# The last chunk of a decoder layer's cross attention: the third chunk's projections in every second step, its gate and its expert slots three steps later, the second sort from step 199 on

## The chip, the cores and the metric

The kernel runs on one core of a Trainium2 chip (trn2), all in float32. The metric is the device time of one launch in microseconds (us). A core has five engines with an instruction queue each: PE (TensorE, matrix products), DVE (VectorE), ACT (ScalarE), POOL (GpSimd) and SP (SyncE, which here only issues DMAs). An engine works its own queue in the order in which it was written, and waits for the others at semaphores.

## What is computed

One decoder layer over 2048 tokens of width 256: linear attention with a residual and a layer norm; cross attention of 16 heads over 1601 keys with a residual and a layer norm; then a mixture of 16 experts, of which each token takes 4, beside a shared one, with a residual and a layer norm.

```python
x = _layernorm(x + _L0_attn_ref(x, ...))
x = _layernorm(x + _L0_xattn_ref(x, ctx_1024, ctx_1024, ...))
x = _layernorm(x + _L0_ffn_ref(x, ...))
# in the cross attention
scores = einsum('bhqd,bhkd->bhqk', Q, K) * scale
out = einsum('bhqk,bhkd->bhqd', softmax(scores), V)
return out @ Wo + bo
# in the mixture
probs = softmax(xf @ gate_w.T)
top_w, top_idx = top_k(probs, 4)        # weights divided by their sum
moe_out = einsum('ted,te->td', eout, combine)
shared = silu(xf @ sw1.T) * (xf @ sw3.T) @ sw2.T
```

## The kernel before

**Steps.** The cross attention is a loop of 208 steps. The queries are cut in four chunks of 512 (`c`), the heads in four groups of four, the keys in 13 tiles (`KT`), so that a chunk has 52 steps and step `s` is tile `kt = s % 13` of group `G = s // 13`. `at` is the step within its chunk; the last chunk is steps 156 to 207, its last group steps 195 to 207. In a step PE makes the scores of four heads (L1531), each into a bank of PSUM of its own, ACT takes their exponentials (L1273), and PE weighs the values with those of two steps before (L1545; L1559 in the last group). The maxima that a softmax needs are found ahead: two "units" of a step are products of PE (L1454) which DVE reduces (L1916, the short last ones of a group L1912). DVE has two such units' banks and PE fills the next only when one has been read. The units run 15 steps ahead, so the last are in step 192. In the last 15 steps DVE has no units.

**Work behind the scores.** What follows the attention of a chunk is spread over the steps of the next one, by the table `EXTRA`: behind the scores of a step, PE does one piece, and ACT copies it out. For the third chunk (`c == CHUNKS - 2`) these are four projections (`proj`, PE L1568, ACT L1169), one for each tile of 128 tokens, the turning of the normalised rows (`x2T`, PE L1576), the gate's products (`logits`, PE L1593) and two counts (`rank`, L1603 and L1606) of how many tokens each expert has got. POOL adds a projection to its rows a step later (`add_attention`, L1002), DVE takes mean and variance another step later (`attended_stats`, L1894 and L1895), POOL makes the inverse deviation (L837), and ACT and POOL normalise two tiles each (POOL L1013). DVE then does the gate in pieces, one in a step (`gate_centre` to `gate_share`), POOL adds up the choices (`third_chosen`), and after the second count DVE works out in which slot of the experts' input each choice goes (`open_more` to `all_slots`, L2143 at its end), and in which order the tiles of slots are to be worked (`order_tiles`, `place_owners`).

**The sort.** POOL writes each token's row to its slots in DRAM with indirect DMAs (`sorted_d`, L853), 128 rows each: 32 for the first two chunks (stage 0) and 16 for the third (stage 1), both within the last chunk's steps, by the table `SORT_AT`; 16 for the last chunk come much later. In POOL's program a scatter of step `s` stands behind a wait for the first score of that step (`ring_full`, `slot(s, 0) + 1`). The 16 of stage 1 go in rounds `j` of four tiles; ahead of each half round stand an iota and a copy (`mark`, L847 and L849) which write the row's place and weight into the rows, and for that first wait until the half's scatters of the round before have landed. POOL also issues the DMA of the order (`write_order`, L919) at step 201.

**The experts' stage.** Its loop has work items `i`, of which the first four are tiles of the shared expert and item 4 is the first of the experts. SP loads that tile's rows from `sorted_d` (L711), with a wait for all scatters of stages 0 and 1 ahead of the first load (L695). PE, at `i == 1`, does the last chunk's projection (L1646), and turns item 4's rows (L1690) right behind it.

Of the kernel before, what the change touches and what calls it, by code (L numbers as in the profile page):

```python
# [20 lines left out]
CHUNKS = SEQ // CHUNK  # L21
TPC = CHUNK // P
# [102 lines left out]
PAIR = 2  # L125
# [19 lines left out]
def decoder_layer(nc, a, out):  # L145
    with ExitStack() as ctx:
# [140 lines left out]
        proj = sb("proj", [P, TPC, DIM])  # L287
# [89 lines left out]
        for c in range(CHUNKS - 1):  # L377
            first = CHUNK_STEPS * (c + 1)
            if c == CHUNKS - 2:
                jobs = ([(12 + t, "proj", t) for t in range(TPC)]  # L380
                        + [(4, "rank", 0), (21, "x2T", 0), (22, "x2T", 1), (23, "logits", 0),
                           (32, "rank", 1)])
            else:
                jobs = ([(PROJ_AT[t], "proj", t) for t in range(TPC)]
                        + [(30, "x2T", 0), (32, "x2T", 1), (34, "logits", 0)])
            for at, what, which_one in jobs:
                assert first + at not in EXTRA
                EXTRA[first + at] = (what, (c, which_one))
# [99 lines left out]
                        NORMED_AT[i + 6] = [t - 1, t]  # L488
        SCATTER_AT = {14 + k: divmod(k, TPC) for k in range(TOPK * TPC)}
        SORT_AT = {}  # L490
        for stage, first, pace in ((0, 166, 0.8), (1, 196, 0.75)):
            for k in range(TOPK * STAGE_TILES[stage]):
                SORT_AT.setdefault(first + int(pace * k), []).append((stage, *divmod(k, STAGE_TILES[stage])))
        assert sum(len(rows) for rows in SORT_AT.values()) == GATE_FIRST * TOPK and max(SORT_AT) < STEPS
# [289 lines left out]
        def _(pool):  # L784
# [231 lines left out]
            for s in range(STEPS):  # L1016
                c, at = divmod(s, CHUNK_STEPS)
                if at == 2 * KT + 9:
                    divide(c, 0)
                if at == 9 and c >= 1:  # L1020
                    divide(c - 1, 1)
                if 1 <= c < CHUNKS - 1:
                    for t in range(TPC):
                        if at == PROJ_AT[t] + 1:
                            add_attention(c - 1, t)
                    if at == 27:
                        inverse_deviation(c_var, c_rstd, c - 1, TPC)
                    if at == 28:
                        normalise(c - 1, range(TPC))
                if c == CHUNKS - 1 and at == 18:  # L1030
                    inverse_deviation(c_var, c_rstd, c - 1, TPC)
                    make_shift(c - 1)
                if c == CHUNKS - 1 and at == 6:
                    first_slots()
                if s in SORT_AT:
                    if s == min(SORT_AT):
                        pool.wait_ge(sorted_cleared, 16 * len(CLEARS))
                    pool.wait_ge(ring_full, slot(s, 0) + 1)
                    for row in SORT_AT[s]:
                        sort_row(*row)  # L1040
                if c == CHUNKS - 1:
                    if 13 <= at < 13 + TPC:
                        add_attention(c - 1, at - 13)
                    if at in (18, 19):
                        normalise(c - 1, (PAIR + at - 18,))
                if c == CHUNKS - 1 and at == 30:
                    third_chosen()
                if s == CHUNK_STEPS * (CHUNKS - 1) + 45:
                    write_order(0)
# [21 lines left out]
        def _(act):  # L1071
# [184 lines left out]
            for s in range(STEPS):  # L1256
# [26 lines left out]
                    copy_logits(arg[0], n)  # L1283
                elif what == "rank":
                    copy_rank(arg[1], n)
                if c == CHUNKS - 1 and at in (19, 20):
                    normalise(c - 1, at - 19)
                if c >= 1 and at == (26 if c == CHUNKS - 1 else 39):
                    exp_gate(c - 1)
            copy_num(CHUNKS * GROUPS - 1)  # L1290

# [540 lines left out]
        def _(dve):  # L1832
# [496 lines left out]
            for s in range(STEPS):  # L2329
# [26 lines left out]
                    if at == 51:  # L2356
                        gate_chosen(c - 1)
                if c == CHUNKS - 1:
                    if 14 <= at < 14 + TPC:
                        attended_stats(c - 1, at - 14)  # L2360
                        if at == 13 + TPC:
                            add_eps(c_var)
                    if at == 25:
                        gate_centre(c - 1)
                    if at == 27:
                        gate_softmax(c - 1)
                    if at == 28:
                        gate_top(c - 1)
                    if at == 29:
                        gate_which(c - 1)  # L2370
                    if at == 30:
                        gate_hot(c - 1)
                    if at == 31:
                        gate_share(c - 1)
                    if at == 6:
                        open_tiles(0)
                    if at == 37:
                        dve.wait_ge(chosen_ready, CHUNKS - 1)
                        dve.wait_ge(slots_ready, 1)
                        open_more(1)  # L2380
                        reach_more(1)
                        slot_of_choice(1)
                        all_slots(1)
                    if at == 42:
                        order_tiles()
                        owners_by_count()
                        place_owners()
                        prepare_last()
# [95 lines left out]
```

## Time and profile before

| | us |
|---|---|
| median of 3 runs | 907.58 |
| lowest and highest | 907.54, 910.18 |
| the profiled execution, time | 907.53 |
| its span, first to last instruction | 905.6 |
| PE busy | 875.7 (97%) |
| DVE busy | 703.0 (78%) |
| ACT busy | 668.4 (74%) |
| POOL busy | 322.3 (36%) |
| granted TensorE clock, mean | 0.994 |

PE is busy nearly throughout, but a busy PE is not PE at its peak: the profile models where a pipelined product ends. In the chain that ended last, PE's lines have 79% of the span, DVE 12% and ACT 5%. The stage that the change touches runs from 625 us (step 168) to about 740 us (the experts' first tile); the experts' stage follows to the end. A step without other work takes 2.47 us up to step 192, and 1.9 to 2.0 us from step 195 on.

### The profile page before, as it was taken

What the parts mean: (1) busy time and instruction counts of PE and PEld (TensorE: products, weight loads), DVE (VectorE), ACT (ScalarE), POOL (GpSimd) and SP (SyncE); (2) the same over time, 40 slices, a digit from 0 to 9 for tenths busy, and PEclk for the clock granted to TensorE, in tenths of its full rate; (3) what the DMA queues carried; (4) which work ended last, traced back from release to release, by engine and by line L of the source; (5) the groups of instructions that cost most, each with busy time, mean ns of one, the idle gap of its engine ahead of it and who ended that gap; (6) DMA issues with size and microseconds to landing.
All of it is one profiled execution on the core that took longest, in us unless ns stands there. A gap on an engine that the chain in (4) does not pass through costs nothing.

```text
span 905.6 us, 19295 instructions
## 1 busy us (share of the span) xinstructions
PE 875.7 (97%) x6987; PEld 501.4 (55%) x6987; DVE 703.0 (78%) x1122; ACT 668.4 (74%) x1491; POOL 322.3 (36%) x385
## 2 busy tenths in 40 slices
PE   8999999999999999999999999999999999999995
PEld 5776776544444444444444444444444367888883
DVE  5336789899999998899998898998889446311587
ACT  4435664378888888888888788888888956677773
POOL 1916787630000001020000020005654644777674
PEclk9999999999999999999999999999999999999997
DMA  9307638403335221011011011011334743466795
GB/s 324 100 1 141 135 100 135 114 26 89 102 96 172 78 71 27 9 26 31 9 26 32 8 25 26 14 26 38 108 112 128 196 124 111 141 173 203 259 327 178
DMA packets 69781, 91.56 MB, mean 101 GB/s; under 512 B 15224, under 2 KB 52602, under 8 KB 69656
## 3 DMA queue, kind: packets, MB, share of 16 engines
q1 hardware_dynamic: 62008, 68.52, 27.0%
q0 software_dynamic: 6928, 18.82, 5.7%
q10 hardware_dynamic: 752, 2.98, 2.0%
q8 instruction: 58, 0.95, 0.5%
q14 instruction: 35, 0.29, 0.1%
HBM read 48.80 MB, written 39.40 MB: 97 GB/s over the span
## 4 chain that ended last, share of the span: by engine, by line
PE 79%; DVE 12%; ACT 5%; issue 2%; POOL 1%; DMA 1%; POOLq 0%; DVEq 0%; ACTq 0%
PE psum L1545 21%; PE psum L1454 17%; PE psum L1531 9%; PE psum L1728 9%; DVE mpart L1916 7%; PE psum L1746 4%; ACT region L1273 3%; PE psum L1374 2%; PE psum L1690 2%; PE psum L1339 2%; PE psum L1505 2%; PE psum L1471 2%; PE psum L1568 1%; PE psum L1347 1%; ACT region L1132 1%
## 5 line engine op out<-in xcount | busy, mean ns | idle before, releaser
L1273 ACT ACTIVATE region<-psum 128x512 f32<-128x512 f32 (+1 forms) x832 | 447.8, 610 | 77.1 <-PE psum L1531 63.3
L1916 DVE TENSOR_REDUCE mpart<-psum 128x2 f32<-128x1024 f32 x384 | 462.0, 1222 | 25.9 <-PE psum L1454 21.3
L1545 PE MATMUL psum<-region 128*32 128x256 f32 (+1 forms) x3120 | 248.8, 390 | 1.8
L1454 PE MATMUL psum<-kstack,qstack 63*128 63x512 f32 (+1 forms) x1024 | 211.2, 441 | 4.9 <-DVE mpart L1916 3.7
L1454 PEld LDWEIGHTS psum<-kstack,qstack 63*128 63x128 f32 x1024 | 88.1, 184 | 173.9 <-issue 123.8
L1531 PE MATMUL psum<-qstack,kstack 64*128 64x512 f32 (+1 forms) x832 | 174.1, 406 | 0.7 <-ACT region L1273 0.7
L1545 PEld LDWEIGHTS psum<-region 128*32 128x32 f32 (+1 forms) x3120 | 64.1, 108 | 107.6 <-issue 83.7
L1531 PEld LDWEIGHTS psum<-qstack,kstack 64*128 64x128 f32 (+1 forms) x832 | 111.2, 181 | 16.2 <-ACT region L1273 13.2
L997 POOL TENSOR_TENSOR attnT<-num_c,den_c 128x512 f32<-128x512 f32 x7 | 9.0, 1281 | 244.6 <-DMA den_c<-den_d 244.4
L928 POOL DMA_INDIRECT given_d<-y_out,x_in x79 | 77.3, 978 | 37.8 <-ACT y_out L1239 25.8
L1728 PE MATMUL psum<-w_all,xT_in 128*128 x316 | 81.6, 381 | 0.9 <-ACT xT_in L1217 0.5
L2284 DVE SCALAR_TENSOR_TENSOR act_h<-silu_h,psum 128x128 f32<-128x128 f32 x95 | 27.2, 287 | 68.6 <-ACT silu_h L1221 68.0
L1728 PEld LDWEIGHTS psum<-w_all,xT_in 128*128 128x128 f32 x316 | 53.9, 190 | 5.5 <-issue 1.3
L853 POOL DMA_INDIRECT sorted_d<-x_rows,slots x48 | 47.6, 992 | 25.5 <-PE psum L1531 14.2
L1132 ACT ACTIVATE region<-psum,small 128x64 f32<-128x64 f32 x128 | 27.9, 329 | 26.8 <-DVE small L1927 26.7
L1746 PE MATMUL psum<-w_all,actT 128*128 x158 | 47.2, 380 | 0.0
L1221 ACT ACTIVATE silu_h<-psum 128x128 f32<-128x128 f32 x85 | 23.6, 278 | 29.7 <-PE psum L1728 29.6
L1239 ACT ACTIVATE y_out<-psum,x_in 128x256 f32<-128x256 f32 x79 | 37.4, 474 | 7.6
L1217 ACT ACTIVATE xT_in<-psum 128x256 f32<-128x256 f32 x95 | 35.7, 377 | 6.5 <-PE psum L1690 6.3
L1912 DVE TENSOR_REDUCE mpart<-psum 128x8 f32<-128x528 f32 x32 | 22.7, 708 | 13.0 <-PE psum L1454 11.6
L1002 POOL TENSOR_TENSOR x_rows<-proj,x_rows 128x256 f32<-128x256 f32 x12 | 8.3, 688 | 65.2 <-ACT proj L1169 65.1
L837 POOL TENSOR_TENSOR rstd<-var_eps,half_neg 128x1 f32<-128x1 f32 (+1 forms) x20 | 13.2, 658 | 49.8 <-DVE var_eps L2002 37.0
(304 smaller groups left out, 1039.2 us busy)
## 6 DMA issues: line engine op xcount, KB each, us to landing
x_in<-sorted_d SPq DMA_DIRECT2D x79, 129.0 KB, 2.3
sorted_d<-x_in SPq DMA_DIRECT2D x6, 1548.0 KB, 7.9
given<-given_d SPq DMA_DIRECT2D x16, 512.0 KB, 5.8
qstack<-qparts_d SPq DMA_DIRECT2D x96, 64.0 KB, 2.3
qparts_d<-region SPq DMA_DIRECT2D x8, 512.0 KB, 3.0
kparts_d<-region SPq DMA_DIRECT2D x4, 800.5 KB, 9.3
kstack<-kparts_d SPq DMA_DIRECT2D x6, 400.2 KB, 10.2
kstack<-kparts_d ACTq DMA_DIRECT2D x6, 400.2 KB, 14.0
```

Source lines behind the costliest of these rows:

```text
L853: pool.indirect_dma_start(out=sorted_d[:, :], out_offset=bass.IndirectOffsetOnAxis(ap=slots[:, t, j:j + 1], axis=0), in_=row, in_offset=No ...
L928: pool.indirect_dma_start(out=given_d[:, :], out_offset=bass.IndirectOffsetOnAxis(ap=x_in[:, v % X_SLOTS, DIM:DIM + 1].bitcast(I32), axis= ...
L1132: ins = act.activation(qexp[:, i % 2, head], bank(i % 2)[:, head], ACT.Exp, bias=small[:, 32 * (i % 2) + h:32 * (i % 2) + h + 1])
L1217: act.activation(xT_in[:, i % 3, :], turn_bank("tile", i)[:, 0:DIM], ACT.Copy).then_inc(xT_copied, 1)
L1239: act.activation(y_out[:, v % Y_SLOTS, :], bank(2 + i % 2)[:, 0:DIM], ACT.Copy, scale=x_in[:, v % X_SLOTS, DIM + 1:DIM + 2]).then_inc(y_co ...
L1273: act.activation(prob[0:rows_of, s % 3, j, :], ring(n)[0:rows_of], ACT.Exp).then_inc(ring_read, 1)
L1454: mm = pe.matmul(bank(unit_bank(u) + side)[:, at * w:(at + 1) * w], qstack[rows_of, buffer(G), p, t * P:(t + 1) * P], kstack[rows_of, g * ...
L1531: pe.matmul(ring(n)[0:r], kstack[rows, g * PAIRS + p, kt * P:kt * P + r], qstack[rows, buffer(G), p, :], start=True, stop=True).then_inc(r ...
L1545: mm = pe.matmul(bank(NUM_BANK)[VW * j:VW * (j + 1), q], vals[0:r, g, kt, j, :], prob[0:r, s % 3, j, q], start=(kt == 0 and half == 0), st ...
L1728: mm = pe.matmul(bank(6 + i % 2)[:, 0:2 * HID], xT_in[:, i % 3, k * P:(k + 1) * P], part_of(kind, v, k), start=(k == 0), stop=(k == DK - 1))
L1746: pe.matmul(bank(2 + i % 2)[:, 0:DIM], actT[:, i % ACT_SLOTS, :], part_of(kind, v, DK), start=True, stop=True).then_inc(y_done, 1)
L1916: dve.tensor_reduce(mpart[:, G % 2, qt, :, p, n], both, X, ALU.max).then_inc(max_read, 1)
```

## The change

It moves work of the third chunk within the last chunk's steps. Nothing is added or left out.

| | before | after |
|---|---|---|
| projections on PE and ACT | steps 168, 169, 170, 171 | 168, 170, 172, 174 |
| POOL adds them | 169 to 172 | 169, 171, 173, 175 |
| DVE's statistics | 170 to 173 | 170, 172, 174, 176 |
| inverse deviation on POOL | 174 | 177 |
| normalising on POOL; on ACT | 174, 175; 175, 176 | 177, 178; 178, 179 |
| `x2T`, `x2T`, `logits` | 177, 178, 179 | 180, 181, 182 |
| DVE's gate, six pieces | 181 to 187 | 184 to 190 |
| `third_chosen` on POOL | 186 | 189 |
| second `rank` | 188 | 191 |
| `open_more` to `all_slots` on DVE | 193 | 196 |
| stage 1 sort on POOL, 16 scatters | 196 + int(0.75 k) | 199 + int(0.55 k) |

`order_tiles` (step 198), `write_order` (201), the load of the order (205) and stage 0's sort (166 to 190) keep their steps.

```diff
-                jobs = ([(12 + t, "proj", t) for t in range(TPC)]
-                        + [(4, "rank", 0), (21, "x2T", 0), (22, "x2T", 1), (23, "logits", 0),
-                           (32, "rank", 1)])
+                jobs = ([(12 + 2 * t, "proj", t) for t in range(TPC)]
+                        + [(4, "rank", 0), (24, "x2T", 0), (25, "x2T", 1), (26, "logits", 0),
+                           (35, "rank", 1)])
...
-        for stage, first, pace in ((0, 166, 0.8), (1, 196, 0.75)):
+        for stage, first, pace in ((0, 166, 0.8), (1, 199, 0.55)):
...
-                    if 14 <= at < 14 + TPC:
-                        attended_stats(c - 1, at - 14)
-                        if at == 13 + TPC:
-                            add_eps(c_var)
-                    if at == 25:
+                    for t in range(TPC):
+                        if at == 14 + 2 * t:
+                            attended_stats(c - 1, t)
+                    if at == 20:
+                        add_eps(c_var)
+                    if at == 28:
                         gate_centre(c - 1)
...
-                    if at == 37:
+                    if at == 40:
                         dve.wait_ge(chosen_ready, CHUNKS - 1)
                         dve.wait_ge(slots_ready, 1)
                         open_more(1)
```

PE's queue from the projection of step 169 to that of step 170, before. L1568 is a projection, L1545 the weighing (half a step's), L1454 the units, L1531 scores:

```order
L1568 MATMUL psum<-wo_c,attnT 32x256 x8
L1545 MATMUL psum<-region 32x256 x4
L1454 MATMUL psum<-kstack,qstack 128x512 x2
L1531 MATMUL psum<-qstack,kstack 128x512 x2
L1545 MATMUL psum<-region 32x256 x4
L1454 MATMUL psum<-kstack,qstack 128x512 x2
L1531 MATMUL psum<-qstack,kstack 128x512 x2
L1568 MATMUL psum<-wo_c,attnT 32x256 x8
```

The same rows of the queue after, from the start of step 170, whose projection is the last row (lines are one further on there):

```order
L1546 MATMUL psum<-region 32x256 x4
L1455 MATMUL psum<-kstack,qstack 128x512 x2
L1532 MATMUL psum<-qstack,kstack 128x512 x2
L1546 MATMUL psum<-region 32x256 x4
L1455 MATMUL psum<-kstack,qstack 128x512 x2
L1532 MATMUL psum<-qstack,kstack 128x512 x2
L1569 MATMUL psum<-wo_c,attnT 32x256 x8
```

Behind the scores of step 169 stands no projection now; the one of step 170 keeps its place, and holds tile 1's instead of tile 2's.

POOL's queue at the start of stage 1's sort, before. L853 is a scatter, L847 and L849 the mark, L919 the DMA of the order; the names in brackets are semaphores, `scattered1a` tells of landed scatters:

```order
L853 DMA sorted_d<-x_rows,slots 10112x258 [waits pool_step]
L853 DMA sorted_d<-x_rows,slots 10112x258
L847 IOTA x_rows 128x2 [waits scattered1b,ring_full]
L849 COPY x_rows<-gates 128x2 [waits pool_step]
L853 DMA sorted_d<-x_rows,slots 10112x258 [waits pool_step]
L853 DMA sorted_d<-x_rows,slots 10112x258 [waits ring_full]
L919 DMA order_d<-place,position 128x2 [waits order_ready]
L847 IOTA x_rows 128x2 [waits scattered1a,ring_full]
```

After:

```order
L853 DMA sorted_d<-x_rows,slots 10112x258 [waits pool_step]
L853 DMA sorted_d<-x_rows,slots 10112x258
L919 DMA order_d<-place,position 128x2 [waits order_ready]
L847 IOTA x_rows 128x2 [waits scattered1b,ring_full]
L849 COPY x_rows<-gates 128x2 [waits pool_step]
L853 DMA sorted_d<-x_rows,slots 10112x258 [waits pool_step]
L853 DMA sorted_d<-x_rows,slots 10112x258
L847 IOTA x_rows 128x2 [waits scattered1a,ring_full]
```

The DMA of the order keeps its step and stands behind six scatters of stage 1, where it stood behind eight.

## Rows read from the trace of the kernel before

**Rows 1.** Busy time by stretch: one without other work, then steps 169 to 181.
```profile
core 0: us, PE busy (x) PEld busy (x) DVE busy (x) ACT busy (x) POOL busy (x), PEclk, DMA share, GB/s
284.33:317.18 32.85, 32.71 (x327) 14.75 (x325) 31.28 (x30) 28.64 (x54) 0.00 (x0) 1.00 0.39 119
629.08:667.96 38.88, 37.53 (x399) 17.73 (x396) 32.55 (x38) 31.25 (x61) 23.96 (x33) 1.00 0.33 100
```
**Rows 2.** The chain that ended last, steps 169 to 179: start, length, what.
```profile
630.79 1.07 PE psum L1568 x16
...
633.59 0.60 ACT numT L1163
...
655.02 0.66 PE psum L1576 x4
...
661.76 0.57 PE psum L1593 x16
```
**Rows 3.** DVE in order of time: start, length, line, operation, idle time before it.
```profile
625.81 2.45 DVE L1916 TENSOR_REDUCE mpart<-psum 128x2 f32<-128x1024 f32 x2
629.28 2.45 DVE L1916 TENSOR_REDUCE mpart<-psum 128x2 f32<-128x1024 f32 x2 [1.02 <-PE psum L1454]
...
645.59 0.42 DVE L1894 BATCH_NORM_STATS2 stats<-x_rows 128x6 f32<-128x256 f32 x1
...
646.34 4.61 DVE L1916 TENSOR_REDUCE mpart<-psum 128x2 f32<-128x1024 f32 x4
650.87 0.24 DVE L1964 RECIPROCAL den<-den 128x16 f32<-128x16 f32 x1
```
**Rows 4.** POOL in order of time, from the inverse deviation to the last normalised tile.
```profile
646.52 1.05 POOL L837 TENSOR_TENSOR rstd<-var_eps,half_neg 128x4 f32<-128x4 f32 x1 [2.31 <-DVE var_eps L2002]
...
653.75 1.22 POOL L1013 TENSOR_SCALAR x_rows<-x_rows,meanvar,rstd 128x256 f32<-128x256 f32 x1
```
**Rows 5.** In order of time: stage 1's slots on DVE; first scores of steps 196, 199.
```profile
703.05 0.17 DVE L2143 CAST slots<-which 128x16 int32<-128x16 f32 x1
...
703.62 0.73 PE L1531 MATMUL psum<-qstack,kstack 64*128 64x512 f32 x4
...
708.97 1.03 PE L1531 MATMUL psum<-qstack,kstack 64*128 64x512 f32 x4
```
**Rows 6.** POOL in order of time, stage 1's sort.
```profile
704.20 0.13 POOL L847 IOTA x_rows<- 128x2 int32 x1 [7.63 <-PE psum L1531]
...
704.86 1.01 POOL L853 DMA_INDIRECT sorted_d<-x_rows,slots  x1 [0.28 <-POOL x_rows L849]
...
707.83 1.00 POOL L853 DMA_INDIRECT sorted_d<-x_rows,slots  x1 [0.28 <-POOL x_rows L849]
...
716.46 0.98 POOL L853 DMA_INDIRECT sorted_d<-x_rows,slots  x1 [1.67 <-PE psum L1531]
717.74 0.96 POOL L919 DMA_INDIRECT order_d<-place,position  x1 [0.30 <-issue]
...
725.69 0.13 POOL L847 IOTA x_rows<- 128x2 int32 x1 [1.04 <-PE psum L1531]
...
731.00 0.98 POOL L853 DMA_INDIRECT sorted_d<-x_rows,slots  x1 [0.42 <-issue]
```
**Rows 7.** L853 over the whole span: from a scatter's issue to its landing.
```profile
DMA to landing us min/median/max: 2.4/2.7/5.3
```
**Rows 8.** L853 in 720.6 to 722 us: the scatter issued at 720.70.
```profile
DMA to landing us min/median/max: 4.9/4.9/4.9
```
**Rows 9.** Busy time by stretch, columns as in Rows 1: the sort, the experts.
```profile
718.00:722.00 4.00, 4.00 (x28) 1.27 (x24) 0.69 (x1) 4.00 (x10) 3.26 (x7) 1.00 0.85 243
728.00:732.00 4.00, 3.56 (x26) 2.31 (x27) 0.68 (x2) 1.91 (x6) 3.21 (x6) 1.00 0.28 99
765.00:850.00 85.00, 85.00 (x471) 71.79 (x471) 22.04 (x81) 60.17 (x204) 61.07 (x65) 1.00 0.57 174
```
**Rows 10.** In order of time: the experts' first loads on SP, first tiles on PE.
```profile
733.68 6.30 SPq L711 DMA_DIRECT2D x_in<-sorted_d  x9
...
736.64 0.38 PE L1690 MATMUL psum<-ident,x_in 128*128 128x128 f32 x2
...
739.77 0.48 PE L1728 MATMUL psum<-w_all,xT_in 128*128 x1 [0.35 <-DVE act_h L2284]
```
**Rows 11.** DMA issues in 733.6 to 736 us: count, size of one, median us to landing.
```profile
x_in<-sorted_d SPq DMA_DIRECT2D x4, 129.0 KB, 2.2
```

More of the change, by code:

```diff
@@ L1029, in _ @@
                         normalise(c - 1, range(TPC))
-                if c == CHUNKS - 1 and at == 18:
+                if c == CHUNKS - 1 and at == 21:
                     inverse_deviation(c_var, c_rstd, c - 1, TPC)
@@ L1041, in _ @@
                 if c == CHUNKS - 1:
[L1042 to L1046, printed above, removed]
+                    for t in range(TPC):
+                        if at == 13 + 2 * t:
+                            add_attention(c - 1, t)
+                    if at in (21, 22):
+                        normalise(c - 1, (PAIR + at - 21,))
+                if c == CHUNKS - 1 and at == 33:
                     third_chosen()
@@ L1285, in _ @@
                     copy_rank(arg[1], n)
-                if c == CHUNKS - 1 and at in (19, 20):
-                    normalise(c - 1, at - 19)
-                if c >= 1 and at == (26 if c == CHUNKS - 1 else 39):
+                if c == CHUNKS - 1 and at in (22, 23):
+                    normalise(c - 1, at - 22)
+                if c >= 1 and at == (29 if c == CHUNKS - 1 else 39):
                     exp_gate(c - 1)
@@ L2358, in _ @@
                 if c == CHUNKS - 1:
-                    if 14 <= at < 14 + TPC:
-                        attended_stats(c - 1, at - 14)
-                        if at == 13 + TPC:
-                            add_eps(c_var)
-                    if at == 25:
+                    for t in range(TPC):
+                        if at == 14 + 2 * t:
[3 more added lines that the diff above has]
+                    if at == 28:
                         gate_centre(c - 1)
-                    if at == 27:
+                    if at == 30:
                         gate_softmax(c - 1)
-                    if at == 28:
+                    if at == 31:
                         gate_top(c - 1)
-                    if at == 29:
+                    if at == 32:
                         gate_which(c - 1)
-                    if at == 30:
+                    if at == 33:
                         gate_hot(c - 1)
-                    if at == 31:
+                    if at == 34:
                         gate_share(c - 1)
```

## The prediction

> **What bounds the kernel now.** I read the busy times by stretch first, then the chain of waits, then single engines in order of time, since the change touches two places that are bound differently.
>
> In the attention loop the stretch with nothing else in it has 13 steps in 32.85 us with PE busy for 32.71 and DVE for 31.28 [rows 1]: PE is the limit and DVE follows closely. Two units of DVE take 2.45 us when it runs just behind PE; when it is late it needs 4.61 for four, so it can make up 2.45 - 2.31 = 0.14 us in a step [rows 3]. The stretch of steps 169 to 181, with the same 13 tiles of keys, takes 38.88 [rows 1]. Of the 6.03 us more, three projections are work of PE: during one DVE sits idle for 1.02 between two pairs of units that are 3.47 us apart [rows 3], so 3 x 1.02 = 3.06. Two turnings at 0.66 and the gate's products at 0.57 [rows 2] are 1.89. What is left, 6.03 - 3.06 - 1.89 = 1.08 us, is stall. The rows name three sources: the copy of `numT` for 0.60 us on ACT's queue in the middle of the chain [rows 2], in a step which also has a projection; statistics that DVE still does when no projection gives it idle time, the last at 645.59 [rows 3]; and `x2T`, which starts at 655.02 [rows 2], right after POOL's last normalised tile is done, 653.75 + 1.22 = 654.97 [rows 4].
>
> At the end of the attention the place to look at is POOL. DVE has the slots of stage 1 ready at 703.05 + 0.17 = 703.22 [rows 5], POOL starts at 704.20 and issues the last scatter at 731.00 [rows 6]. SP's first load of an expert's tile goes out at 733.68, and PE turns that tile at 736.64, behind other work and without a wait of its own [rows 10]. A load takes 2.2 us to land [rows 11], so the rows are there at about 735.9. The sort has **0.8 us of slack** before PE waits for it. From 765 to 850 us PE is busy for 85.00 of 85.00 [rows 9], so what PE loses at the start of the experts' stage is lost at the end.
>
> **The projections spread out.** PE's, ACT's and POOL's instructions are the same in number and length, so only the 1.08 us of stall can be won. The statistics of tiles 0, 1 and 2 now fall in steps 170, 172 and 174, each with a projection, where DVE has 1.02 us idle; one takes about 0.7 with its second half and what is between (645.59 to 646.34 with `add_eps` [rows 3]). The fourth falls in step 176 with no cover; it delays DVE by 0.75, and the reciprocal adds its 0.24 [rows 3]. Before, those of steps 172 and 173 had no projection beside them. I count 0.4 us won. The `numT` step, 170, keeps its projection, but ACT no longer comes from a step with another: 0 to 0.3 won, I take 0.1. The turning stays four steps behind the statistics with the same POOL work between, two normalised tiles and three scatters, 646.52 to 654.97 [rows 4]; I take nothing there. The gate's products now stand in step 182 instead of 179, where DVE's units are short; the cover that this gave is gone, which costs about 0.05. Sum: **0.45 us won**. Bounds: 1.1 if all stall goes, 0.4 lost if POOL's chain comes later than the turning.
>
> **Gate and slots three steps later.** The same DVE work runs into the same full steps; its cover is the 0.14 us that DVE can make up in a step, and it moves by three steps with it. The one new neighbour is the reciprocal of step 188, now in the middle: 0 to 0.24 lost [rows 3], taken as 0. `open_more` moves from step 193 to 196, but behind step 192 DVE has nothing to wait for in between and its queue order there is unchanged, so the slots still come at about 703.2. If the second count were late this would slip; it stands at 191, and DVE reaches it only behind the units of 192.
>
> **The sort from step 199.** POOL now stands at the first score of step 199 where it stood at that of 196. Those start at 708.97 and 703.62 [rows 5], and the mark began 704.20 - 703.62 = 0.58 behind [rows 6]. So it begins at 709.55, and the first scatter at 709.55 + 0.66 = 710.21, **5.35 us later**. The closer pace cannot catch up with POOL's own speed: a pair of scatters with its mark takes 707.83 - 704.86 = 2.97 us [rows 6]. Seven pairs, one more issue (1.30) and the order's DMA (717.74 - 716.46 = 1.28) are 23.37 us; the last scatter is issued at 733.58 at the earliest, against 731.00. Before, the same work took 26.14, so it stood still for 2.77: a gap of 1.67 instead of 0.30 ahead of 716.46, which the profile puts down to a score that is long past, and so does not explain; a mark that waited 1.04 at 725.69; and 0.4 of smaller pieces [rows 6]. That mark needs the scatter of 720.70 landed, and 720.70 + 4.9 = 725.6 is when it was [rows 8].
>
> What of these 2.77 comes back decides the case. Landings are slow while SP's loads of the experts' weights fill the DMA engines, 0.85 busy in 718 to 722 us, and quick when these are done, 0.28 in 728 to 732 [rows 9]; over all scatters they take 2.4 to 5.3 [rows 7]. The later scatters now fall mostly in the quiet part, but those issued at 716.2 and 717.5 fall into the full one, and the mark due at 722.9 needs both. At 4.9 it would begin at 722.4, at 5.3 at 722.8, so just in time; the full stretch may hold them longer since two queues meet there. I take 1.0 us of standing still, near the one wait whose cause the rows show, with bounds of 0 and 2.8.
>
> So the last scatter is issued 2.58 + 1.0 = 3.6 us later, PE's wait is 3.6 - 0.8 = 2.8. Of that the 0.35 us that PE then waited for DVE at 739.77 [rows 10] is absorbed, since DVE gets ahead meanwhile: 2.45 us lost.
>
> The Trainium skill, DMA: Bandwidth & Descriptors, section "Anatomy of one DMA — SWDGE (gpsimd) path", gives 2.0 us plus the bytes over 436 GB/s for a DMA that POOL issues. For 129 KB that would be about 2.3 us, an estimate by that page; by it no mark would wait, and the time would be that of the first rival below. The trace agrees at the minimum, 2.4, and not in the full stretch, 4.9 and 5.3 [rows 7, 8].
>
> **The sum.** The profiled execution took 907.53 us (span 905.6), 0.05 under the median of the three runs, so it stands for them. 907.53 - 0.45 + 2.45 = **909.5 us**.
>
> **Rivals.**
> First, the sort stands still nowhere, because its later part is out of the loads' way. Then the loss is 2.58 - 0.8 - 0.35 = 1.43, and the time 907.53 - 0.45 + 1.43 = 908.5. For it speaks the busy share of 0.28 behind 728 us, against it the unexplained gap.
> Second, slower: POOL stands still as long as before. Place: the marks and scatters between 716 and 726 us. Price 2.77 instead of 1.0: 907.53 - 0.45 + 4.2 = 911.3. It decides once PE's first expert tile starts over 4 us late. For it speaks that the weights' loads keep their steps, and that one gap came with no landing or score to wait for.
> Third, faster: the stalls of the attention go wholly, 1.1 here and up to 1.0 in the gate's steps, while the sort is as in the first rival: 907.53 - 2.1 + 1.43 = 906.9. Against it: the fourth statistics and the gate have no more cover than before.
> Fourth, it doesn't do what it says: the sort isn't bound by its step but by something else that keeps it at 704 us, so that only the 0.45 remains: 907.1. The wait for step 199's score stands in POOL's queue, so I give it little.
>
> **How the numbers follow.** Forecast, 1.0 us still, between 908.8 and 910.4: 0.43. First rival 0.20, second 0.22, third 0.08, fourth 0.03; 0.04 for what I don't see. The range of 907.0 to 911.6 leaves out about the third rival's far end and the tail above the second. A measurement of this kernel tells about 0.3%, 2.7 us, from no change, so that slower means above 910.3 and faster below 904.9. Slower: the second rival, the forecast's upper end and half of the unseen, 0.30. Faster: 0.04, since even the third rival doesn't reach it. Same: 0.66.
>
> **What would show each step.** In the trace after: steps 169 to 181 hold three projections and both turnings, without the gate's products; DVE's idle time of about 1 us should come with every second pair of units, with statistics in it. The turning at step 180 should follow POOL's second tile closely. POOL's first scatter of stage 1 should stand at about 709.8, shortly behind the scores of step 199, the last at 733 to 736. PE's first L1690 on `x_in` should show a wait for a DMA, which it has not now. From 765 us on all should be shifted by the same amount. The forecast is wrong if the first scatter of stage 1 isn't later by 5 us, if PE shows no wait there, or if the experts' stage takes up the shift, which it could only by idle time of PE that the rows don't show.

## The result, and the profile after

The changed kernel took 912.41 us (median of 6 runs, 911.83 to 913.69), the kernel before, run beside it, 908.52 (6 runs, 907.54 to 910.18): a ratio of 1.0046, interval 1.0036 to 1.0057. That is 3.9 us slower, where 2.0 were forecast, outside the range given. The profiled execution of the changed kernel took 912.02 us, with a span of 910.2 against 905.6: 4.6 us more.

All but little of the difference lies at one place. PE's first expert tile starts 3.66 us later than before, the third 5.05, and from 765 us on every tile 4.57. Ahead of the sort nothing is lost: step 199 starts at 709.03, where it stood at 708.97 [rows 5].

The change's first part, busy time by stretch with the columns of [rows 1], steps 169 to 181, and then the same stretches as [rows 9]:

```profile
629.31:667.02 37.71, 36.75 (x382) 17.29 (x380) 32.86 (x38) 31.46 (x60) 24.03 (x33) 1.00 0.35 108
```
```profile
718.00:722.00 4.00, 4.00 (x28) 1.27 (x24) 0.68 (x1) 4.00 (x10) 2.89 (x5) 1.00 0.83 250
722.00:726.00 4.00, 4.00 (x28) 1.11 (x24) 0.00 (x0) 4.00 (x11) 2.28 (x4) 1.00 0.29 95
728.00:732.00 4.00, 3.51 (x25) 2.26 (x26) 0.68 (x2) 1.92 (x6) 3.27 (x5) 1.00 0.19 68
765.00:850.00 85.00, 85.00 (x472) 71.99 (x471) 23.14 (x85) 60.10 (x204) 60.70 (x64) 1.00 0.55 163
```

The thirteen steps are 38.88 - 37.71 = 1.17 us shorter, but 0.57 of it are the gate's products, which now stand in step 182. The last line is why a loss at 740 us stays: PE has no idle time from 765 to 850, as before. The lines from 718 to 726 us show the busy share of the DMA engines fall from 0.83 to 0.29 at 722, and POOL less busy behind it (2.28 of 4.00 against 2.89): it stands still there.

POOL in order of time, to be read beside [rows 6]:

```profile
709.60 0.13 POOL L847 IOTA x_rows<- 128x2 int32 x1 [14.27 <-PE psum L1532]
...
710.26 1.01 POOL L853 DMA_INDIRECT sorted_d<-x_rows,slots  x1 [0.28 <-POOL x_rows L849]
...
718.85 0.96 POOL L919 DMA_INDIRECT order_d<-place,position  x1 [0.30 <-issue]
...
724.10 0.13 POOL L847 IOTA x_rows<- 128x2 int32 x1 [0.98 <-DMA sorted_d<-x_rows,slots]
...
735.44 0.97 POOL L853 DMA_INDIRECT sorted_d<-x_rows,slots  x1 [0.30 <-issue]
```

The gap of 1.67 us ahead of 716.46 is gone, and one mark waits 0.98 for a landing. From the first scatter to the last it takes 25.18 us, of which the prediction's bare chain is 733.58 - 710.21 = 23.37: POOL stands still for 1.8.

Then SP's loads and PE, to be read beside [rows 10]:

```profile
738.14 3.86 SPq L711 DMA_DIRECT2D x_in<-sorted_d  x6
```
```profile
735.83 1.03 PE L1647 MATMUL psum<-wo_c,attnT 128*128 128x256 f32 x4
740.30 0.41 PE L1691 MATMUL psum<-ident,x_in 128*128 128x128 f32 x2 [3.45 <-DMA x_in<-sorted_d]
740.55 1.18 PE L1729 MATMUL psum<-w_shared,xT_in 128*128 128x256 f32 x4
741.52 0.42 PE L1737 MATMUL psum<-ident,act_h 128*128 128x128 f32 x1
741.74 0.64 PE L1691 MATMUL psum<-ident,x_in 128*128 128x128 f32 x2
742.16 1.92 PE L1729 MATMUL psum<-w_shared,xT_in 128*128 128x256 f32 x4
```

PE now waits 3.45 us for the DMA that brings `x_in`. What follows was in nobody's sum: the same four products that take 1.03 us in an undisturbed tile take 1.92. Busy time of PE alone by stretch (length, busy time and count, granted clock, DMA share, GB/s) says why:

```profile
740.00:741.00 1.00, 0.70 (x5) 1.00 0.97 275
741.00:742.00 1.00, 1.00 (x6) 0.65 0.28 92
742.00:744.00 2.00, 2.00 (x7) 0.50 0.78 216
744.00:745.00 1.00, 1.00 (x6) 0.64 0.36 112
745.00:746.00 1.00, 1.00 (x6) 1.00 0.78 186
```

The granted clock falls from 1.00 to 0.50, from 2.4 to 1.2 GHz, shortly after PE has resumed, and is back by 745. The same stretch before:

```profile
736.00:746.00 10.00, 9.40 (x54) 1.00 0.61 168
```

### The profile page after: what moved, and what is told of

The parts are those of the page before. It is cut to its first block, busy times and chain, and to the rows that moved or that the text cites. A ratio compares the mean times of both kernels' runs of the same rounds, so it can differ in the third digit from the quotient of the medians.

```text
span 910.2 us, 19293 instructions
## 1 busy us (share of the span) xinstructions
PE 878.0 (96%) x6987; PEld 503.5 (55%) x6987; DVE 703.4 (77%) x1122; ACT 668.9 (73%) x1491; POOL 322.3 (35%) x385
## 4 chain that ended last, share of the span: by engine, by line
PE 80%; DVE 10%; ACT 3%; issue 3%; DMA 2%; POOL 2%; POOLq 0%; SPq 0%; DVEq 0%; ACTq 0%
PE psum L1546 21%; PE psum L1455 17%; PE psum L1532 9%; PE psum L1729 9%; DVE mpart L1917 6%; PE psum L1747 4%; PE psum L1375 2%; PE psum L1691 2%; PE psum L1340 2%; PE psum L1506 2%; PE psum L1472 2%; PE psum L1569 1%; PE psum L1348 1%; ACT region L1133 1%; POOL sorted_d L853 1%
## 5 line engine op out<-in xcount | busy, mean ns | idle before, releaser
L853 POOL DMA_INDIRECT sorted_d<-x_rows,slots x48 | 47.7, 994 | 22.8 <-PE psum L1532 10.8
L1691 PE MATMUL psum<-ident,x_in 128*128 128x128 f32 x158 | 30.8, 277 | 3.7 <-DMA x_in<-sorted_d 3.4
```

The lines of the kernel that those rows point to most:

```text
L853: pool.indirect_dma_start(out=sorted_d[:, :], out_offset=bass.IndirectOffsetOnAxis(ap=slots[:, t, j:j + 1], axis=0), in_=row, in_offset=No ...
L1691: mm = pe.transpose(turn_bank("tile", i)[:, k * P:(k + 1) * P], rows[:, k * P:(k + 1) * P], ident[:, :])
```

## The experiments

Thirteen runs were made, in four groups, each group on one chip beside the kernel before. "Shift" is by how much a tile of the experts' stage starts later than in the trace of the kernel before.

**The parts apart.** First the attention's part alone, the sort where it was:

```diff
-        for stage, first, pace in ((0, 166, 0.8), (1, 199, 0.55)):
+        for stage, first, pace in ((0, 166, 0.8), (1, 196, 0.75)):
```

> The changed kernel with stage 1's sort back at steps 196 + int(0.75 k); projections, gate and slots stay where the change put them. Theory (the later start of the sort makes the loss): PE's first expert tile has no wait for a DMA, PE's granted clock stays at full from 740 to 746 us, and the time is that of the kernel before less the little that spreading wins, 0.0 to 0.4 us less. Rival (the projections and the gate, moved, disturb the loop or the experts' stage): the time stays near that of the changed kernel, 3 to 4 us over the kernel before.

Measured: 908.0 us (12 runs), ratio 1.0000, interval 0.999 to 1.001. PE waits nowhere for `x_in`, the clock stays at 1.00, the shift is -0.15. The sort behaves as it did before:

```profile
713.73 0.99 POOL L853 DMA_INDIRECT sorted_d<-x_rows,slots  x1 [0.28 <-POOL x_rows L849]
716.33 0.98 POOL L853 DMA_INDIRECT sorted_d<-x_rows,slots  x1 [1.61 <-PE psum L1532]
...
726.25 0.13 POOL L847 IOTA x_rows<- 128x2 int32 x1 [1.43 <-DMA sorted_d<-x_rows,slots]
```

Then the sort's part alone, on the kernel before: `(1, 199, 0.55)` in place of `(1, 196, 0.75)`.

> The kernel before with only the sort's line changed: 199 + int(0.55 k). Theory: the whole loss is here, PE waits 3.3 to 3.7 us for its first expert tile, and the time is 4.0 to 4.8 us over the kernel before. Rival: half or less of the loss, up to 2 us, the rest comes from the moved work.

Measured: 913.47 us (6 runs), ratio 1.0056, interval 1.0039 to 1.0074. The whole loss comes from the sort. It is more than I expected, 5.6 us over the kernel before instead of 4.0 to 4.8. Its trace shows the wait and the clock again, both larger (I had put the wait at 3.3 to 3.7):

```profile
741.44 0.66 PE L1690 MATMUL psum<-ident,x_in 128*128 128x128 f32 x2 [4.24 <-DMA x_in<-sorted_d]
741.89 1.91 PE L1728 MATMUL psum<-w_shared,xT_in 128*128 128x256 f32 x4
```
```profile
741.00:744.00 3.00, 2.56 (x8) 0.50 0.59 175
744.00:746.00 2.00, 2.00 (x8) 0.50 0.62 184
```

The clock is at 0.50 for some 6.8 us here, about twice as long as in the first trace, and the shift rises by 2.3 us behind the first tile, from 4.80 to 7.13, where it rose by 1.4 there.

Then the pace alone, on the kernel before: `(1, 196, 0.55)`.

> The kernel before with stage 1's sort at 196 + int(0.55 k), so the closer pace without the later start. Theory: POOL issues at its own speed, not the table's, so the last scatter is issued within 1 us of 731.0 us and the time is within 0.3 us of the kernel before, since the sort has slack there. Rival (the pace matters by itself, since the steps' waits held the old sort back): the last scatter comes 2 to 3 us sooner; if it matters to the time, that is shorter by up to 0.5 us.

Measured: 908.7 us (12 runs), ratio 1.0003, interval 0.9993 to 1.0012. In the trace everything stands 1.55 us later from before the cross attention's first step on, which the edit can't cause (more on this below); taken off, the last scatter is issued at 731.1 against 731.00. The closer pace gives nothing, as POOL is at its own speed at either, and it costs nothing. The gap ahead of the eighth scatter stays at 1.69.

So the late start of the sort is the cause of the loss. What lies between 2.0 forecast and 3.9 measured was next: the clock.

**The clock.** If it falls because PE idles, work that nobody needs in that idle time should keep it up. Fourteen more products stand ahead of the first expert tile's wait. They write the PSUM bank of that tile, whose own products overwrite their result:

```diff
+                if kind == "expert" and v == 0:
+                    for n in range(FILL):
+                        pe.matmul(turn_bank("tile", i)[:, 0:DIM], ident[:, :], wo_c[:, n % DK, :], start=True, stop=True)
```

> The changed kernel with 14 products of PE added (identity by an attention weight, 128x256, about 0.216 us each, 3.0 us in all) into the bank of the first expert tile, ahead of its wait; their result is overwritten. PE is then busy through most of the 3.45 us that it waits. Theory A (the wait costs its own length and, behind it, a granted clock of 0.5 for some 3 us): the clock stays at 1.0 behind the wait and the time is 1.0 to 1.5 us under the changed kernel, 3.0 to 3.5 over the kernel before. Theory B (the slower products behind the wait are of no account because something else, DVE or the loads, bounds there): the time is that of the changed kernel within 0.3 us.

Measured: 913.27 us (6 runs), ratio 1.0055, interval 1.004 to 1.007. The fill took 6.0 us and not 3.0, as each product is two of 0.21; so it held PE up itself, by 5.83 us at the first tile, and the total is neither what theory A nor what theory B gave. But from 735 to 746 us PE is busy without a break and the clock stays at 1.00, and the shift goes down from 5.83 to 5.31 instead of up:

```profile
735.00:746.00 11.00, 11.00 (x56) 1.00 0.45 122
```

With seven (`FILL = 7`, 3.0 us) the fill fits into the wait:

> The changed kernel, with 7 more products in front of the first expert tile's wait (they write a PSUM tile that nobody reads; nothing of the result changes). In the trace of the kernel with 14 of them, 14 took 6.0 us, so these 7 take about 3.0 us of the 3.45 us in which TensorE waits for x_in. Theory A (behind that wait the granted clock falls, 0.50 for some 3 us, and the tiles run slower): with 7 products TensorE still waits about 0.4 us at 740.3, the first tile starts where it did in the changed kernel, but the granted clock stays at 1.00, and the tiles from 765 us stand 1.0 to 1.5 us ahead of the changed kernel's: median 910.9 to 911.4 where the changed kernel has 912.4. Rival (the clock has nothing to do with that wait, or the time is lost elsewhere behind the wait): the stretch 741 to 745 us shows 0.50 again, or the tiles keep their 4.6 us: the time of the changed kernel within 0.3 us. Second rival: the products end too late and push the first tile: the shift of the first tile is over 4.0 us.

This and the next three were one group, on a chip on which the kernel before itself took 935.8 us. In all four traces PE stands idle again and again in the experts' stage. Its busy time between 765 and 850 us in the last of the four:

```profile
765.00:850.00 85.00, 74.47 (x372) 0.94 0.45 132
```

The records put most of these waits down to DVE's `act_h` in one trace and to nothing that the profile shows ("issue") in another, and name no DMA, so their cause is open. The totals of these four say less than their traces up to 765 us. With seven products: 937.52 us (12 runs), ratio 1.0018, interval 1.0005 to 1.0030; PE waits 1.02 us, the clock stays at 1.00, and the shift of the tiles goes from 5.72 to 5.23.

> The kernel before with the second sort's slots at step 197 + int(0.65 k) in place of 196 + int(0.75 k); the projections stay as before. The sort starts one step (2.3 to 1.7 us) later and is issued a little closer. Theory A (the sort's last link is POOL's chain of issues; slack of 0.8 us before PE waits; a wait lets the clock fall only when it is long enough): last scatter 731.9 to 732.7, x_in lands at 737.0 to 738.2, PE waits 0.4 to 1.6 us at its first tile and the clock stays at 1.00: 0.0 to +1.2 us over the kernel before. Rival B (any wait there brings the 0.50 of the granted clock): +1.5 to +2.6 us. Rival C (the change of the pace gives back what the start takes, as an earlier sort finds other landings): within 0.3 us of before with no wait at all.

The kernel before with `(1, 197, 0.65)`: 937.33 us (12 runs), ratio 1.0019, interval 1.0009 to 1.0030. The traced execution can't answer the question of the sort: in it the attention's last steps lost 5.2 us, with one standstill of PE among them, so that the experts' stage came that much later anyway; a mark then waited 2.75 us and PE still only 0.35. But that standstill says something on the clock. PE alone, in stretches around 674 us, where the longest gap is 1.38 us:

```profile
673.00:675.00 2.00, 0.62 (x8) 1.00 0.36 128
675.00:676.00 1.00, 1.00 (x10) 0.67 0.09 25
676.00:678.00 2.00, 2.00 (x14) 0.50 0.11 23
678.00:679.00 1.00, 1.00 (x8) 0.62 0.39 111
```

The same fall, at a place that no edit touches.

> The kernel before with the second sort's slots at step 198 + int(0.6 k): starts two steps later. Theory A (start, POOL's chain, slack 0.8): last scatter 733.5 to 734.5, PE waits 1.8 to 3.2 us at its first expert tile. If the granted clock falls behind a wait of this length as it did behind 3.45 us: +2.5 to +4.0 us over the kernel before. If it doesn't: +1.4 to +2.8 us. Rival (the clock fell in the changed kernel by something else than the wait): the clock shows 1.00 or falls at a place that no wait precedes.

The kernel before with `(1, 198, 0.6)`: 938.88 us (6 runs), ratio 1.0048, interval 1.0033 to 1.0063. Here too PE had a gap in attention, 1.84 us ahead of 722.93, and the clock was at 0.50 from 724 to 726. At the first expert tile PE waited 1.05 us, and the clock stayed up. Its rival, a fall that no wait precedes, isn't seen in this trace; more on that below. My band of 1.8 to 3.2 us for the wait at the tile was missed, because the gap in attention had taken some of it.

Last on this chip, the weights. The loads of experts 10 and 11 go out at key tiles 11 and 12 of the last group, in the changed kernel:

```diff
-                           (15, ((1, 15), (4, 8), (5, 9), (8, 10), (9, 11)))):
+                           (15, ((1, 15), (4, 8), (5, 9), (11, 10), (12, 11)))):
```

> The changed kernel, with the weight loads of experts 10 and 11 issued at key tiles 11 and 12 of the last group in place of 8 and 9, so that they don't move beside the first scatters. Theory A (POOL's standstill of 0.98 us at the mark at 724.10 and the late landings come from the weights that move beside the scatters): the landings of the first half take 2.4 to 3 us, the standstill at the mark goes, the last scatter is issued 0.9 to 1.8 us earlier, PE's wait of 3.45 us is shorter by as much, and the time 0.9 to 2.5 us under the changed kernel. Rival B (POOL's standstills don't hang on the loads): last scatter within 0.3 us of 735.44, and the same time. Rival C (the moved loads collide with the second half of the scatters and with x_in): the first half is quicker, the second slower, x_in lands as late or later, time the same or up to 2 us over the changed kernel.

Measured: 938.94 us (5 runs), ratio 1.0039, interval 1.0027 to 1.0052. The mark that had waited 0.98 for a landing has no wait on a DMA, but POOL still needs 737.60 - 712.13 = 25.47 us from the first scatter to the last, no less than the 25.18 of the first trace; in its neighbour with seven products it needs 25.75. PE waits 4.06 us. Rival B describes it best: the standstills change place and their sum stays. That moving these loads shortens them is not borne out.

The two fit together to price the clock: in both, the first tile comes 4.2 us late against the tiles of the shared layer just ahead of it (1.52 to 5.72, 1.93 to 6.16). Behind 4.06 us of idle time the clock falls, and the shift rises to 7.25 and ends at 7.10; with the fill it doesn't fall, and the shift goes to 5.23. Against their own start that is 5.17 and 3.71: 1.46 us apart. The moved loads differ as well, so the next group has the clean pair.

**The same again, side by side.** The changed kernel unaltered, with seven products, and with three (1.46 us of work):

> The changed kernel once more, unaltered, as the partner of the next two on the same chip. From the first trace: PE waits 3.45 us for x_in, the granted clock then falls to 0.50 for some 3 us, the tiles end 4.6 us behind the kernel before. The medians should differ by 3.5 to 5 us; if the experts' stage of this chip is bound by the loads of the weights, by less.

> The changed kernel with 7 more products in front of the first expert tile's wait (nothing of the result changes), now beside the changed kernel itself. Theory A (the fall of the clock behind PE's wait costs about 1.4 us): clock at 1.00 from 740 to 750 us, first tile within 0.3 us of the changed kernel's, later tiles 1.2 to 1.6 us ahead of it, median 1.0 to 1.6 us under it. Rival (the clock's fall costs nothing in the end, as PE catches up elsewhere): tiles from 765 us within 0.4 us of the changed kernel's, medians alike.

> The changed kernel with 3 such products, about 1.3 us of the 3.45 us: PE still idles for about 2.1 us. In the traces so far the clock stayed at 1.00 behind waits of 1.02 and 1.05 us and fell behind 1.38, 1.84 and everything longer. If that holds, it falls here as in the changed kernel, and the time is that of the changed kernel within 0.5 us. Rival (a fall in proportion to the wait): about half of the 1.4 us is saved, and the stretch at 0.50 is shorter.

Measured beside a kernel before of 908.28 us: unaltered 912.09 (6 runs, ratio 1.0039, 1.0026 to 1.0053), with seven 911.49 (6 runs, 1.0032, 1.0020 to 1.0044), with three 910.94 (8 runs, 1.0031, 1.0020 to 1.0042). The intervals overlap, so these totals don't tell the three apart. The traces contradict two of the three expectations. With three products PE waits 1.90 us, and the clock stays at 1.00, where I expected the fall. In the unaltered kernel PE waits 3.00 us, and the clock doesn't fall either:

```profile
740.13 0.41 PE L1691 MATMUL psum<-ident,x_in 128*128 128x128 f32 x2 [3.00 <-DMA x_in<-sorted_d]
740.38 1.03 PE L1729 MATMUL psum<-w_shared,xT_in 128*128 128x256 f32 x4
...
741.57 1.03 PE L1729 MATMUL psum<-w_shared,xT_in 128*128 128x256 f32 x4
```

This is the clean pair: two executions of the same kernel, with the fall (first trace) and without. The shift of the first and third tile is 3.66 and 5.05 with it, 3.49 and 3.52 without. So **the fall costs 1.4 us** when it comes and is as long as there. It need not come. With seven products the clock stays at 1.00 behind a wait of 0.38, but as the unaltered kernel had no fall in this group, its tiles aren't the expected 1.2 to 1.6 us ahead.

The trace of the unaltered kernel has a second surprise. Its tiles run at a shift of 2.94 until 880 us, and then at 3.84; with seven products it is 3.19 and 4.21. PE waits there for `act_h` and `xT_in`, which queue on DVE and ACT while DVE also adds up the last outputs (`given`). In the first trace and with three products nothing is lost there. What decides it is open.

**Is the fall typical?** Two more, again side by side:

> The changed kernel, unaltered, as the partner of the next run. In the 12 executions so far its mean granted clock was 0.991 to 0.994 (mean 0.9929), where the kernel before had 0.9949 over 15. If a typical execution has the fall behind PE's wait, this is 0.993 again, and the median is 3.5 to 4.5 us over the kernel before. In the rival (the fall is rare, as in the second trace, which had none) the clock is that of the kernel before, and the median nearer to 3 us over it.

> The changed kernel with 3 more products in front of the first expert tile's wait, again. If the fall of the clock is what they take away: mean granted clock over the executions 0.9945 to 0.9955, the median 0.8 to 1.6 us under the changed kernel's, no fall in the trace between 740 and 750 us. If they only moved work about: the same clock and the same median within 0.4 us.

Measured beside a kernel before of 907.82 us: unaltered 913.29 (5 runs, ratio 1.0058, 1.0045 to 1.0071), with three products 912.30 (6 runs, 1.0056, 1.0041 to 1.0070). The unaltered kernel is 5.5 us over the kernel before, more than the 3.5 to 4.5 expected; it waits 3.35 us and has the fall, and a second one at 169 us, of which more below. The one with three products waits only 1.96 us and has it too, where its first trace, with 1.90, had none:

```profile
740.00:741.00 1.00, 0.78 (x4) 0.79 0.86 242
741.00:743.00 2.00, 2.00 (x8) 0.50 0.55 142
```

So three products don't keep it away each time. Their median is 1.0 us under the unaltered kernel's, as expected, but not their clock, and the two ratios are nearly the same. The clocks of all executions say more than single traces. The unaltered kernel has 0.991 to 0.994 in its 17, mean 0.9928. The kernel before has means of 0.9950 (23 executions), 0.9949 (15) and 0.9951 (11). With seven or fourteen products, on the chips that are alike, 12 executions have a mean of 0.9950; with three, 14 have 0.9938, between. A deficit of 0.0022 over 911 us is 2.0 us of full clock. The rows of the fall in the first trace add up to 0.35 + 1.00 + 0.36 = 1.7. So most executions of the changed kernel should have the fall. This is worked out from means, and only three of them were traced, two with it; the mean of a single execution decides nothing, since the clock is at 0.50 at the end of every kernel too, for 7.5 us in one trace and 10.2 in another.

**A fall without a new wait.** The 1.55 us of the trace with the pace alone come from the clock too. PE's busy time at 169 us in that trace and, last, in the kernel before:

```profile
169.00:170.00 1.00, 1.00 (x3) 0.64 0.00 0
170.00:172.00 2.00, 2.00 (x5) 0.50 0.00 0
172.00:173.00 1.00, 1.00 (x5) 0.66 0.00 0
```
```profile
170.00:172.00 2.00, 2.00 (x8) 1.00 0.00 0
```

The gaps of PE just ahead are 0.56 and 0.63 us, in both kernels alike, and its busy time from 165 to 169 us is 2.81 of 4.00 in both; one had the fall and the other not. The last trace of the unaltered kernel has it as well, and its tiles come 1.4 us later from there. It may be what makes some executions of the kernel before slower: 14 of the 49 took over 908.6 us, with a mean clock of 0.9939, the other 35 have 0.9955. No trace was taken of one of the 14, so this isn't shown.

No variant beats both kernels. The fastest is the attention's part alone, and it can't be told from the kernel before.

## Why the prediction was wrong

By its own terms, for the first trace (forecast, found):

```
                                    forecast    found
attention by step 199                 -0.45     +0.06
PE's first tile behind that           +2.8      +3.60
clock behind the wait                  0        +1.39
absorbed behind the wait              -0.35     -0.48
sum                                   +2.0      +4.57
```

**The path was right up to PE's wait.** The first scatter was put at 710.21 and came at 710.26. PE's first L1691 shows a wait for a DMA, all tiles from 765 us are shifted by the same amount, and the loss comes from the sort alone, as the two halves showed (1.0000 and 1.0056). The second rival's test, PE's first expert tile over 4 us late, was not met (3.66), though the time was past that of this rival. The slack was as read: the last scatter is issued 4.44 us later, the tile starts 3.66 later, 0.8 less.

**Step that failed first: nothing follows the wait.** I priced PE's wait as its length less what DVE absorbs, as if the engine came back as it went. The clock adds 1.4 us, the largest single error; with the next one, 0.8, it takes the sum from 909.5 to 911.7, past the range; the 0.5 of the attention makes it 912.2, and 0.1 more absorbed 912.1, against 912.02 in the profiled execution. The trace of before held a warning that I passed over. Its mean clock of 0.994 is no even loss: the clock is 1.00 up to 895 us and 0.50 from 896 to the end, where PE mostly idles. Two products there take 1.19 us, where the same two take 0.67 before the fall:

```profile
894.27 0.67 PE L1746 MATMUL psum<-w_shared,actT 128*128 128x256 f32 x2 [0.42 <-DVE sums L2294]
896.86 1.19 PE L1746 MATMUL psum<-w_shared,actT 128*128 128x256 f32 x2 [1.92 <-DVE sums L2294]
```
```profile
896.00:900.00 4.00, 1.19 (x2) 0.50 0.62 197
```

So the price of a product at 0.50 could be read there. How long the clock would stay down behind a wait of some 3 us, and whether it would fall at all, could not. A prediction that makes such a new wait on the engine that bounds the kernel has to carry a term for the clock, with a bound. I had none.

**Step mis-sized: the standstill of POOL.** I took 1.0 us of the 2.77, the first trace has 1.8: 0.98 at the mark at 724.10, and the rest in pieces of up to 0.3 us. My reasoning on the landings was half right: the mark's landing was late, but later than the 5.3 that I took as the worst. This trace records none of them; in the second trace of the same kernel the same scatter took 6.1 to land. The pieces I had seen in the rows of before too, as 0.4 in all, and let go with the rest. The unexplained gap of 1.67 did go, as I had half counted on. It returns at 1.61 and 1.69 in the kernels with the sort at 196, and never in those at 199. What it is stays open. So does what sets the sum: the expectation that moving the weights' loads would shorten it fell.

**Step mis-sized: attention.** I took 0.45 us. From the start of step 169 to that of step 195 the change wins 72.61 - 72.23 = 0.38. But step 195 takes 2.14 us where it took 1.93: PE, now earlier, waits there for the load of the last group's maxima. The page's row of the score line shows it, where before it named only ACT:

```profile
L1532 PE MATMUL psum<-qstack,kstack 64*128 64x512 f32 (+1 forms) x832 | 174.3, 407 | 0.5 <-DMA qstack<-max_d 0.3
```

The weights of step 195's first score wait for that load in both kernels, and SP issues it at 699.80 where it was 699.78, so an earlier PE gains nothing there. At step 199 there are 0.17 us left, and 0.11 to 0.15 in seven more traces of kernels with this part (those of the chip with 935.8 us left out). The first trace lay 0.23 us behind by step 169 already, where nothing was changed yet, so it shows +0.06. The gain was real, and a wait for a DMA stands where half of it was lost again. My 0.1 for the step with `numT` was not won either: step 170 takes 4.03 us in both kernels. Where DVE was to do its statistics under the projections, it does: 1.02 and 1.09 us of its idle time come with the first two projections, 0.56 and 0.55 with the others. DVE in order of time:

```profile
629.51 4.92 DVE L1917 TENSOR_REDUCE mpart<-psum 128x2 f32<-128x1024 f32 x4 [1.02 <-PE psum L1455]
634.35 0.42 DVE L1895 BATCH_NORM_STATS2 stats<-x_rows 128x6 f32<-128x256 f32 x1
634.80 0.18 DVE L1896 BATCH_NORM_AGGREGATE meanvar<-stats 128x2 f32<-128x6 f32 x1
636.07 4.85 DVE L1917 TENSOR_REDUCE mpart<-psum 128x2 f32<-128x1024 f32 x4 [1.09 <-PE psum L1455]
```

**The gate moved** cost nothing, as forecast: the slots came in time, and POOL's first instruction was released by the score of step 199.

**The absorption** was 0.35 by the one gap that I had seen. From the third tile to 765 us it is 0.48 in the first trace and 0.40 to 0.60 in nine others; with the loads moved it is 0.15, in the second trace with three products 0.77.

For the measured medians the sum closes less neatly. They differ by 3.9, 3.8 and 5.5 us in the three groups that had the changed kernel, the single traces by 4.6, 3.9 and 5.8 in span, with the kernel before's single trace as their base. What differs among them is the clock's fall behind the wait, the 0.9 us near 881, and the fall at 169 us in the last, which puts its tiles 1.4 us later.

## What to carry to other kernels

A wait that you put on TensorE where it bounds the kernel can cost more than its length: look whether the granted clock falls behind it, and carry a term for that in the sum, with a chance. The mean clock of a page says nothing of where it was lost: read it by stretch, the kernel's last microseconds too. Work that is moved later ahead of a hand-over should be moved by no more than its slack: here 0.8 us of slack met a delay of 5.35, and a closer pace could give nothing back, since the issuing engine ran at its own speed already. A gain ahead of a load's landing is only worth what that landing leaves of it.

## What the runs showed of the hardware

- TensorE's granted clock fell from 1.00 to 0.50 (2.4 to 1.2 GHz) at gaps of 1.38, 1.84, 1.96, 3.35, 3.45, 4.06 and 4.24 us. It stayed there for some 3.4 us each time but the last, which cost 1.4 us at the changed kernel's first tiles, and for 6.8 us at the last, which cost 2.3. Behind 0.38, 1.02, 1.05, 1.90 and 3.00 it did not fall. In the experts' stage of the chip with 935.8 us it fell at 2.71 and 4.14 too, and not behind 1.76 and 2.02. Behind gaps of 0.56 and 0.63 it fell at 169 us in two traces and not in the others. So the length of the last gap alone doesn't decide, and the same kernel can show either.
- In every trace the clock is at 0.50 in the last 7.5 to 11.2 us of the kernel, where PE mostly idles; in the kernel before from 895.6 to 905.6 us.
- In two traces several engines stood still together: PE for 1.38 us ahead of 674.91, ACT for 1.19 and DVE for 1.15, at a place that no edit touches; and PE for 1.84 ahead of 722.93, ACT for 1.93 and POOL for 1.31, in the middle of a moved sort. The records name no cause outside them.
- On one of the four groups' chips every kernel took 3% longer (the kernel before 935.8 us against 907.8 to 908.5). PE was busy for 74.5 of 85 us in the experts' stage of one trace, where it is busy throughout elsewhere; the cause is open. Whether a delay of PE's start counts for less in the total there is not settled: two kernels whose first tile came 4.2 us later against the tile ahead have ratios of 1.0018 and 1.0039, and a third with 1.2 us has 1.0048.
- A product of 128x256 f32 operands is 0.43 us of PE, as two records of 0.21.
